# A new order for the attention stage of an attention and expert kernel: loads by turns, experts chosen from tile 0, identity products at the start

## The chip, the cores and the metric

The kernel runs on one core of a Trainium2 chip. The metric is the device time of one execution in microseconds (us); the time shown is the median of three executions.

## What is computed

For each of two batches, x (512 tokens by 1024) passes a cross attention without softmax and then a mixture of experts, each added to x:

```
x = x + matmul(fake_quant(layernorm(x)), fake_quant(ctx))       # ctx: 1024 x 1024 per batch, 8 bit codes
h = layernorm(x)
ratio  = mean|h[tokens 153..511]| / mean|h[tokens 0..152]|        # one number per batch
scores = softmax([h, ratio] @ gate_w + gate_b)                    # 3 experts
top_val, top_idx = top_k(scores, 2), top_val normalised to sum 1
for i in 0, 1:
    j = top_idx[:, 0, i]                                          # the expert that TOKEN 0 of the batch picks
    x = x + top_val[..., i] * (act_j(h @ w1[j] + b1[j]) @ w2[j] + b2[j])
```

Two facts matter for the change. The experts of a batch are those of its token 0, which lies in token tile 0; the other tokens' scores are only used as weights of the outputs. And the ratio needs the absolute values of all tokens of the batch.

## The kernel before, in words

Each batch has four tiles of 128 tokens. All queues are written out by hand, one list of calls for each engine, and semaphores tie them together; an engine takes its list strictly in order.

The **first stage** computes the attention. SyncE loads eight tiles of x (`load_x(i)`, tiles 4 to 7 are batch 1) and sixteen chunks of the context (`load_ctx(c)`, chunks 8 to 15 are batch 1), 512 KB each, through one queue in the order written. A tile of x gets its statistics on VectorE (`x_stats`), its reciprocal deviation on GpSimd (`x_rstd`), its scales on VectorE (`q1_scales`), is turned into codes (`quant_x`), is transposed by TensorE (`transpose_q1`) and is copied out of PSUM (`load_q1T`). A chunk of context is turned into codes by `quant_ctx`. The tables `CTX_ORDER`, `Q1_ORDER`, `Q1T_ORDER` and `H_ORDER` say which engine does which tile. `codes_product(b, t, k)` is two matmuls of 512 columns, for token tile t and context chunk k; `column_sums` and `row_sums` feed `col_term`, `row_term` (ScalarE) and `split_col_term`, `split_row_term` (VectorE), whose result `add_terms(b, t)` adds at the end of a tile. `attn_add(b, t)` (VectorE) then adds the tile to x.

For batch 0 the same stage prepares the experts: `h_stats`, `h_power`, `h_offset`, `h_tile`, `transpose_h`, `split_h` (high part, ScalarE), `h_lo` (low part, VectorE), `sum_h` (absolute values, ScalarE), `sum_abs` and `router_bias` (the ratio), `gate_product(0, t)` (16 small matmuls a tile: the router's logits), `gate_logits`, `gate_turn`, `turned_scores`, `score_steps`, `gate_exp`, `choose_experts`. SyncE waits for the choice, loads `w1` of the chosen expert in quarters of two chunks, and each chunk is split into a rounded part (`w_hi_chunk`, ScalarE) and a rest (`w_lo_chunk`, VectorE) before TensorE may use it.

The **second stage** is a loop over p = 0 to 3 (batch 0 first and second expert, batch 1 first and second expert). Each p has eight blocks f of 24 matmuls (line 1655) and seven products i of 2 x 12 matmuls (line 1623), all of 512 columns. Block f = 0 takes the four chunks of the first two quarters of w1 in turn, six matmuls for each chunk. Beside them VectorE splits weights and activations, adds the second bias (`bias_add`, from `b2row`), adds results (`result`), and for batch 1 computes the router by dot products (`gate_dot(n)`, one for each tile and expert, 12 in all) since batch 1's h is transposed only late: `second_h_tile(t)` (GpSimd) writes h into `b2row`, once both biases of batch 0 have been added, and TensorE transposes it (`transpose_h(1, 0)`) in front of block f = 6 of p = 1. GpSimd also issues the DMAs that add weight regions to each other (`t3_sum`, `t2_sum`, `t4_sum`).

## Time and the profile before

| | before |
|---|---|
| median of 3 runs | 399.26 us (398.29 to 399.35) |
| profiled execution: span, and its own time | 398.3 us, 398.3 us |
| TensorE busy | 384.2 us, 96% |
| VectorE busy | 319.4 us, 80% |
| ScalarE busy | 194.6 us, 49% |
| GpSimd busy | 75.4 us, 19% |
| DMA moved | 66.98 MB, mean 168 GB/s |

The profile is one execution. The span runs from the first to the last instruction. A busy time adds up the time in which an engine works; the records of matmuls overlap, so that the distance from one start to the next says more of TensorE's pace than the length of a record. PE is TensorE, PEld its weight loads, DVE VectorE, ACT ScalarE, POOL GpSimd, SPq the queue of SyncE.

### The profile page before, as it was taken

The numbers are of one execution on the slowest core, as the hardware profiler recorded it, in microseconds if no ns is written. First come the engines' busy times: TensorE is split into PE (matmuls) and PEld (weight loads), VectorE is DVE, ScalarE is ACT, GpSimd is POOL, SyncE is SP. The second block draws the span as 40 slices with busy tenths as digits, with TensorE's granted clock in tenths as the row PEclk, the third lists the DMA queues.
The fourth block names the chain that finished last, engine by engine and source line by source line (L and its number), as shares of the span: only waits on it lengthen the run. The fifth ranks groups of instructions, "written<-read, shape, count | busy, mean of one in ns | idle before, by whom it ended". The sixth has DMA issues, their size and how long they took to land.

```text
span 398.3 us, 5246 instructions
## 1 busy us (share of the span) xinstructions
PE 384.2 (96%) x1860; PEld 302.7 (76%) x1860; DVE 319.4 (80%) x529; ACT 194.6 (49%) x253; POOL 75.4 (19%) x94
## 2 busy tenths in 40 slices
PE   1999999999999999999999999999999999999996
PEld 1345656888888888888888888888888888888885
DVE  8689967999599799898899995654997864639972
ACT  3477745274247635372755833344475244424720
POOL 8647500352110001063103001030000010110000
PEclk9999999999999999999999999999999999999999
DMA  8997019719654676728002898965065884550112
GB/s 300 412 410 305 3 50 375 264 21 282 121 105 137 233 229 226 180 39 158 15 0 90 304 291 281 248 118 96 0 209 172 262 275 88 105 106 2 53 53 107
DMA packets 27437, 66.98 MB, mean 168 GB/s; under 512 B 2160, under 2 KB 2192, under 8 KB 27280
## 3 DMA queue, kind: packets, MB, share of 16 engines
q1 hardware_dynamic: 23888, 54.01, 38.8%
q0 software_dynamic: 3456, 12.58, 16.5%
q8 instruction: 15, 0.25, 0.3%
q14 instruction: 14, 0.11, 0.1%
q10 hardware_dynamic: 64, 0.02, 0.0%
HBM read 49.83 MB, written 4.19 MB: 136 GB/s over the span
## 4 chain that ended last, share of the span: by engine, by line
PE 89%; DVE 6%; POOL 1%; issue 1%; ACT 1%; POOLq 0%; ACTq 0%
PE ps L1655 44%; PE ps L1623 38%; PE ps L1415 4%; DVE bn L840 2%; DVE xres L911 2%; PE ps L1449 1%; POOL ctxq L453 1%; PE ps L1403 1%; DVE hT_lo L920 0%; DVE ctxq L858 0%; POOL ctxq L446 0%; DVE q L874 0%; POOL q_rstd L427 0%; DVE q_bias L1147 0%; PE ps L1484 0%
## 5 line engine op out<-in xcount | busy, mean ns | idle before, releaser
L1037 DVE TENSOR_TENSOR w_lo<-raw,w_hi 128x1024 fp32r<-128x1024 f32 x88 | 103.4, 1218 | 2.6 <-ACT w_hi L688 2.4
L688 ACT ACTIVATE w_hi<-raw 128x1024 fp32r<-128x1024 f32 x88 | 87.8, 1052 | 34.5 <-DVE raw L1050 18.0
L1655 PE MATMUL ps<-hT_hi,w_hi 128*128 128x512 f32 x256 | 100.0, 391 | 0.0
L1655 PE MATMUL ps<-hT_lo,w_hi 128*128 128x512 f32 x256 | 99.6, 389 | 0.0
L1655 PE MATMUL ps<-hT_hi,w_lo 128*128 128x512 f32 x256 | 99.6, 389 | 0.0
L1623 PE MATMUL ps<-w_hi,a_hi 128*128 128x512 f32 x224 | 87.4, 390 | 0.0
L1623 PE MATMUL ps<-w_hi,a_lo 128*128 128x512 f32 x224 | 87.2, 389 | 0.0
L1623 PE MATMUL ps<-w_lo,a_hi 128*128 128x512 f32 x224 | 87.1, 389 | 0.0
L776 ACT ACTIVATE act_f<-ps,b1T 128x512 f32<-128x512 f32 x32 | 22.1, 689 | 112.4 <-PE ps L1655 112.4
L523 POOL DMA_DIRECT2D raw<-raw x24 | 21.3, 1038 | 193.0 <-DMA raw<-in_L_ffn_w_dram 137.9
L1655 PEld LDWEIGHTS ps<-hT_hi,w_hi 128*128 128x128 f32 x256 | 48.1, 188 | 10.6 <-issue 0.4
L1655 PEld LDWEIGHTS ps<-hT_hi,w_lo 128*128 128x128 f32 x256 | 48.1, 188 | 10.1
L1655 PEld LDWEIGHTS ps<-hT_lo,w_hi 128*128 128x128 f32 x256 | 48.1, 188 | 9.7
L1054 DVE TENSOR_TENSOR a_lo<-act_f,a_hi 128x256 fp32r<-128x256 f32 x32 | 15.2, 474 | 47.0 <-ACT a_hi L782 47.0
L1623 PEld LDWEIGHTS ps<-w_hi,a_lo 128*128 128x128 f32 x224 | 42.0, 188 | 8.8
L1623 PEld LDWEIGHTS ps<-w_hi,a_hi 128*128 128x128 f32 x224 | 42.1, 188 | 8.6
L1623 PEld LDWEIGHTS ps<-w_lo,a_hi 128*128 128x128 f32 x224 | 42.1, 188 | 8.6
L1415 PE MATMUL ps<-ctxq,q1T 128*128 128x512 f16 x128 | 32.9, 400 | 1.6 <-DVE xres L911 1.1
L1119 DVE SCALAR_TENSOR_TENSOR xres<-ps,minus_gate,xres 128x512 f32<-128x512 f32 x32 | 23.3, 744 | 8.1 <-PE ps L1623 8.1
L1415 PEld LDWEIGHTS ps<-ctxq,q1T 128*128 128x128 f16 x128 | 11.7, 101 | 18.0 <-issue 5.8
L716 ACT ACTIVATE a_hi<-act_f 128x1024 fp32r<-128x1024 f32 x16 | 16.9, 1058 | 10.8 <-PE ps L1623 10.8
L1103 DVE SCALAR_TENSOR_TENSOR xres<-b2row,gate,xres 128x1024 f32<-128x1024 f32 x16 | 20.5, 1279 | 0.0
(155 smaller groups left out, 367.9 us busy)
## 6 DMA issues: line engine op xcount, KB each, us to landing
raw<-in_L_ffn_w_dram SPq DMA_DIRECT2D x64, 512.0 KB, 5.2
raw<-raw POOLq DMA_DIRECT2D x24, 512.0 KB, 6.6
raw<-in_ctx_dram SPq DMA_DIRECT2D x16, 512.0 KB, 11.8
xres<-in_x_dram SPq DMA_DIRECT2D x8, 512.0 KB, 9.7
out_dram<-xres SPq DMA_DIRECT2D x16, 256.0 KB, 4.1
b2row<-in_L_ffn_b_dram SPq DMA_DIRECT2D x4, 512.0 KB, 6.0
gate_rows<-in_L_ffn_gate_w_dram SPq DMA_DIRECT2D x1, 1536.0 KB, 17.7
small<-in_L_xattn_x_scale_dram ACTq DMA_DIRECT2D x2, 0.0 KB
```

What stands on the lines that cost most here:

```text
L523: G.dma_start(region(into)[:, 2 * c:2 * c + 2, :], region(other)[:, 2 * c:2 * c + 2, :], accum_op=ALU.add).then_inc(done, 16)
L688: nc.scalar.activation(w_hi[n % SLOTS][:, 2 * c:2 * c + 2, :], region(q)[:, 2 * c:2 * c + 2, :], ACT.Copy).then_inc(w_hi_ready, 1)
L716: nc.scalar.activation(dst[:], src, ACT.Copy).then_inc(late_hi_ready, 1)
L776: nc.scalar.activation(act_f[:, f, :], ps[:, G1_BANK + f % 2, :], EXPERT_ACT[ee], bias=bias)
L840: last = V.bn_stats(bn[:, n, c, :], src[:, c * H:(c + 1) * H])
L1037: V.tensor_tensor(w_lo[n % SLOTS][:, 2 * c:2 * c + 2, :], region(n % QUARTERS)[:, 2 * c:2 * c + 2, :], w_hi[n % SLOTS][:, 2 * c:2 * c + 2, ...
L1054: V.tensor_tensor(a_lo[f // TT][:, f % TT, :], act_f[:, f, 0:2 * P], a_hi[f // TT][:, f % TT, :].bitcast(F32), ALU.subtract).then_inc(a_lo ...
L1103: V.scalar_tensor_tensor(out=xt, in0=b2row[:], scalar=gate[:, p * TT + t:p * TT + t + 1], in1=xt, op0=ALU.mult, op1=ALU.add).then_inc(b2_u ...
L1119: V.scalar_tensor_tensor(out=xt, in0=ps[:, bank + j, :], scalar=signed[:, p * TT + t:p * TT + t + 1], in1=xt, op0=ALU.mult, op1=ALU.add).t ...
L1415: T.matmul(ps[:, ATT_BANK[b][t] + c, :], q1T[b][:, k, t * P:(t + 1) * P], ctxq[b][:, k, c * H:(c + 1) * H], start=k == 0, stop=False)
L1623: last = T.matmul(ps[:, bank + j, :], a[slot][:, k, tok], v[w][:, k, :], start=fresh and n == 0, stop=n == 3 * TT - 1, skip_group_check=True)
L1655: last = T.matmul(ps[:, G1_BANK + f % 2, :], w[q % SLOTS][:, k % TT, fs], h[:, k, :], start=n == 0, stop=n == 3 * KT - 1)
```

## The change

- **Loads.** Context chunks and x tiles go by turns: x0 x1 c0 x2 c1 x3 c2 c3 x4 c4 x5 c5 c6 c7 x6 x7 c8 to c15. Before: x0 to x3, c0 to c7, x4 x5, c8 c9, x6 x7, c10 to c15.
- **Experts from tile 0.** For batch 0 only tile 0's logits are computed by `gate_product` and turned (one matmul in `gate_turn` where there were four). The scores of the tiles 1 to 3, and `gate_values`, move into the second stage and use `gate_dot(b, t, e)`: nine dots in p = 0 for batch 0, three in p = 1 (tile 0 of batch 1) and nine in p = 2. Before there were three in p = 0 and nine in p = 1, all for batch 1.
- **Bias.** `bias_add` of the first expert of a batch moves into the blocks f = 0 and 1 of the second expert, whose own bias follows in f = 2 and 3. `b2row` of the second expert is loaded behind all of its weights, and waits for the first bias to be added.
- **Statistics of batch 1's h** (`h_stats(5..7)`) move from p = 0 to p = 1, and GpSimd's `h_power(4..7)` with them, behind the weight sums of p = 0 and ahead of those of p = 1.
- **Identity products.** `keep_busy(n)` issues n matmuls of 128 columns of the identity with ones; their result is not used. They stand ahead of the scales (34), the gate weights (30), and around the first two transposes (8, 10, 24).
- **Order.** The lists of all engines in the first stage, the PSUM banks and the waits that guard them are written anew. The work of the second stage is otherwise the same.

The diff, cut to its core (the banks, their waits and the scores' slices are left out):

```diff
-CTX_ORDER = {"act": [5, 8, 10, 11, 15, 14],
-             "dve": [2, 4],
-             "pool": [0, 1, 3, 6, 7, 9, 12, 13]}
-Q1_ORDER = {"act": [0, 1, 3, 4],
-            "dve": [2, 7],
-            "pool": [5, 6]}
-Q1T_ORDER = {"act": [0, 1, 2, 5, 4, 7],
-             "dve": [3, 6]}
+CTX_ORDER = {"act": [1, 3, 5, 8, 12, 15],
+             "dve": [2, 7],
+             "pool": [0, 4, 6, 10, 11, 9, 14, 13]}
+Q1_ORDER = {"act": [0, 1, 6, 7],
+            "dve": [2],
+            "pool": [3, 4, 5]}
+Q1T_ORDER = {"act": [0, 1, 2, 3, 4, 5, 6, 7],
+             "dve": []}
 H_ORDER = {"act": [],
-           "dve": [],
-           "pool": [0, 1, 2, 3]}
+           "dve": [3],
+           "pool": [0, 1, 2]}
...
-EARLY_DOTS = 3
+DOTS_BEFORE = [NE * (TT - 1), NE * TT, NE * (2 * TT - 1)]
...
+FIRST, OTHERS = slice(0, 1), slice(1, TT)
+WARM_BANK = 5
+WARM_FIRST = 34
+WARM_NEXT = 30
+WARM_GAP = 8
+WARM_WAIT = 10
+WARM_LAST = 24
...
+            def load_b2(p, e):
+
+                if p:
+                    sp.wait_ge(b2_used, TT * p)
+                if p == TOP_K:
+                    sp.wait_ge(hT_ps, B * TT)
+                sp.dma_start(b2row[:], b2[bass.ds(e, 1), :].to_broadcast([P, D])).then_inc(b2_in, 16)
...
             load_x(0)
             load_x(1)
+            load_ctx(0)
             load_x(2)
+            load_ctx(1)
             load_x(3)
-            load_ctx(0)
-            load_ctx(1)
             load_ctx(2)
             load_ctx(3)
+            load_x(4)
             load_ctx(4)
+            load_x(5)
             load_ctx(5)
             load_ctx(6)
             load_ctx(7)
-            load_x(4)
-            load_x(5)
+            load_x(6)
+            load_x(7)
             load_ctx(8)
             load_ctx(9)
-            load_x(6)
-            load_x(7)
             load_ctx(10)
             load_ctx(11)
...
+                if p % TOP_K == 0:
+                    load_b2(p, e)
                 load_w1(p, 2, e)
                 load_w1(p, 3, e)
                 for q in range(4):
                     load_w2(p, q, e)
+                if p % TOP_K:
+                    load_b2(p, e)
                 if p == TOP_K:
                     store_results(sp, 0)
...
+            t3_sum(0)
+            t2_sum(0)
+            t4_sum(0)
             for t in range(TT):
                 h_power(TT + t)
                 h_offset(TT + t)
...
-            t3_sum(0)
-            t2_sum(0)
-            t4_sum(0)
             t3_sum(1)
             second_h_tile(0)
             t2_sum(1)
...
+            load_bias()
+            load_q1T(2)
+            load_q1T(3)
             quant_ctx(5)
-            quant_x(3)
-            load_q1T(2)
+            row_term(0)
             col_term(0)
-            row_term(0)
             quant_ctx(8)
-            quant_x(4)
-            quant_ctx(10)
-            quant_ctx(11)
+            load_q1T(4)
+            load_q1T(5)
+            quant_x(6)
+            quant_x(7)
+            load_q1T(6)
+            quant_ctx(12)
             sum_h(0, 0)
-            load_q1T(5)
+            load_q1T(7)
             split_h(0, 0)
-            load_bias()
             sum_h(0, 1)
-            load_q1T(4)
             split_h(0, 1)
+            gate_logits()
             sum_h(0, 2)
-            quant_ctx(15)
             split_h(0, 2)
-            quant_ctx(14)
             sum_h(0, 3)
             split_h(0, 3)
-            gate_logits(0)
-            load_q1T(7)
-            gate_exp(0)
+            quant_ctx(15)
             row_term(1)
             col_term(1)
+            gate_exp(0, FIRST, 1)
             w_hi_chunk(0, 0)
             w_hi_chunk(0, 1)
             w_hi_chunk(1, 0)
...
                     dve.wait_ge(b2_in, 16 * p + 16)
-                    dve.wait_ge(y2_done, 2 * NP * p)
+                    dve.wait_ge(y2_done, 2 * NP * (p // TOP_K * TOP_K + 1))
...
                     n = 2 * NP * p + 2 * i + j
-                    if i == 0:
+                    if i == 0 and p % TOP_K:
                         dve.wait_ge(b2_used, TT * p + TT)
+                    elif i == 0:
+                        dve.wait_ge(dots_done, NE * (TT * (p // TOP_K + 1) - 1))
                     elif i in (1, 4, 5):
...
-            term_constants()
             x_stats(2)
+            x_stats(3)
             quant_ctx(2)
-            x_stats(3)
-            quant_ctx(4)
             gate_weights()
             q1_scales(2, 2)
             quant_x(2)
-            load_q1T(3)
             x_stats(4)
             x_stats(5)
+            term_constants()
+            q1_scales(4, 2)
+            quant_ctx(7)
+            split_row_term(0)
+            x_stats(6)
             split_col_term(0)
-            split_row_term(0)
-            q1_scales(4, 2)
+            x_stats(7)
             attn_add(0, 0)
+            q1_scales(6, 2)
+            attn_add(0, 1)
             h_stats(0)
-            attn_add(0, 1)
             attn_add(0, 2)
             h_stats(1)
             attn_add(0, 3)
+            h_stats(2)
             h_lo(0, 0)
-            h_stats(2)
             h_stats(3)
             h_lo(0, 1)
-            x_stats(6)
-            x_stats(7)
+            h_tile(3)
             h_lo(0, 2)
-            q1_scales(6, 2)
-            quant_x(7)
             tokens_abs(0)
             h_lo(0, 3)
-            load_q1T(6)
             router_bias(0)
+            split_row_term(1)
             turned_scores()
-            score_steps()
+            score_steps(FIRST)
+            split_col_term(1)
             choose_experts(0)
-            split_row_term(1)
-            split_col_term(1)
             attn_add(1, 0)
             attn_add(1, 1)
+            h_stats(4)
+            attn_add(1, 2)
             w_lo_chunk(0, 0)
             w_lo_chunk(0, 1)
             w_lo_chunk(1, 0)
             w_lo_chunk(1, 1)
-            attn_add(1, 2)
-            gate_values(0)
             attn_add(1, 3)
-            h_stats(4)
             for p in range(PAIRS):
                 q = QUARTERS * p
-                if p == 1:
...
+                        if f < 2:
+                            gate_dot(0, 1, 2 * f)
+                        if f == 0:
+                            gate_dot(0, 1, 1)
+                        elif f == 1:
+                            gate_dot(0, 2, 0)
+                            gate_dot(0, 2, 1)
+                        elif f == 3:
+                            gate_dot(0, 2, 2)
+                        elif f == 4:
+                            gate_dot(0, 3, 0)
+                        elif f == 5:
+                            gate_dot(0, 3, 1)
+                            gate_dot(0, 3, 2)
+                    elif p == TOP_K:
+                        if f == 0:
+                            gate_dot(1, 1, 0)
+                        elif f == 1:
+                            gate_dot(1, 1, 1)
+                            gate_dot(1, 1, 2)
+                        elif f == 2:
+                            gate_dot(1, 2, 0)
+                            gate_dot(1, 2, 1)
+                        elif f == 3:
+                            gate_dot(1, 2, 2)
+                            gate_dot(1, 3, 0)
+                        elif f == 4:
+                            gate_dot(1, 3, 1)
+                        elif f == 5:
+                            gate_dot(1, 3, 2)
+                    elif f < 2:
+                        bias_add(p - 1, 2 * f)
+                        bias_add(p - 1, 2 * f + 1)
+                    elif f < 4:
+                        bias_add(p, 2 * f - 4)
+                        bias_add(p, 2 * f - 3)
+                    if p % TOP_K == 0 and f == 5:
+                        dot_scores(p // TOP_K, OTHERS)
+                        score_steps(OTHERS)
+                    if p == 1:
+                        if f < 3:
+                            h_stats(TT + 1 + f)
+                        elif f == 5:
+                            gate_dot(1, 0, 0)
+                            gate_dot(1, 0, 1)
+                            gate_dot(1, 0, 2)
                     if f == 3:
                         w_lo_quarter(q + 4)
                     elif f == 4:
...
                         router_bias(1)
-                        dot_scores()
-                        score_steps()
...
                                         start=n == 0, stop=n == 2 * KT - 1)
                         n += 1
-                if t == TT - 1:
-                    last.then_inc(logitT_ps, 1)
+                last.then_inc(logitT_ps, 1)
 
             def sum_abs(b):
 
...
+            def keep_busy(n):
+
+                for _ in range(n):
+                    T.matmul(ps[:, WARM_BANK, 0:P], ident_b[:], ones_b[:], start=True, stop=True)
+
             pe.wait_ge(const_ready, 7)
+            keep_busy(WARM_FIRST)
             pe.wait_ge(scales_in, 16 * 4)
             T.matmul(ps[:, CONST_BANK, 0:4], ones[0:1, :], small[0:1, 0:4], start=True, stop=True
                      ).then_inc(scales_ps, 1)
+            keep_busy(WARM_NEXT)
             turn_gate_weights()
+            keep_busy(WARM_GAP)
             transpose_q1(0)
+            keep_busy(WARM_WAIT)
             transpose_q1(1)
+            turn_bias()
+            keep_busy(WARM_LAST)
             codes_product(0, 0, 0)
             codes_product(0, 0, 1)
             codes_product(0, 0, 2)
             codes_product(0, 1, 0)
+            codes_product(0, 1, 2)
             codes_product(0, 1, 1)
             codes_product(0, 0, 3)
-            codes_product(0, 1, 2)
+            transpose_q1(2)
             codes_product(0, 1, 3)
-            codes_product(0, 1, 4)
+            transpose_q1(3)
             column_sums(0, 0)
             column_sums(0, 2)
+            codes_product(0, 2, 0)
+            codes_product(0, 2, 4)
             codes_product(0, 0, 4)
+            row_sums(0)
...
+            transpose_q1(4)
             codes_product(0, 2, 2)
+            add_terms(0, 0)
...
+            codes_product(0, 3, 0)
+            codes_product(0, 3, 7)
             add_terms(0, 2)
+            transpose_q1(6)
...
-            transpose_q1(4)
-            transpose_q1(5)
+            transpose_q1(7)
             transpose_h(0, 0)
-            turn_bias()
+            codes_product(1, 0, 0)
+            codes_product(1, 2, 0)
+            codes_product(1, 2, 4)
+            codes_product(1, 0, 2)
+            transpose_h(0, 1)
+            gate_product(0, 0)
+            codes_product(1, 2, 3)
+            transpose_h(0, 2)
+            codes_product(1, 2, 2)
+            codes_product(1, 0, 3)
+            codes_product(1, 0, 4)
+            transpose_h(0, 3)
+            codes_product(1, 2, 1)
+            codes_product(1, 0, 1)
+            row_sums(1)
+            codes_product(1, 2, 6)
+            column_sums(1, 0)
+            column_sums(1, 2)
+            sum_abs(0)
+            column_sums(1, 4)
+            column_sums(1, 6)
+            codes_product(1, 0, 5)
+            codes_product(1, 0, 6)
+            gate_turn()
             codes_product(1, 1, 0)
-            codes_product(1, 1, 1)
             codes_product(1, 1, 2)
             codes_product(1, 1, 3)
+            codes_product(1, 1, 1)
             codes_product(1, 1, 4)
+            codes_product(1, 0, 7)
+            add_terms(1, 0)
             codes_product(1, 1, 5)
...
+            add_terms(1, 1)
+            codes_product(1, 3, 0)
+            codes_product(1, 2, 7)
             codes_product(1, 2, 5)
-            codes_product(1, 2, 6)
-            add_terms(1, 0)
-            codes_product(1, 2, 7)
-            add_terms(1, 1)
+            codes_product(1, 3, 3)
             add_terms(1, 2)
-            codes_product(1, 3, 0)
+            codes_product(1, 3, 5)
+            codes_product(1, 3, 4)
+            codes_product(1, 3, 6)
+            codes_product(1, 3, 7)
             codes_product(1, 3, 1)
             codes_product(1, 3, 2)
```

## Rows read from the trace of the kernel before

**Rows 1.** The page: the span.
```profile
span 398.3 us, 5246 instructions
```

**Rows 2.** Busy time by stretches: first stage, p = 0, p = 1 (stretch, its length, engines, PEclk, DMA).
```profile
12.07:64.08 52.01, 50.04 (x363) 26.14 (x364) 42.20 (x99) 32.07 (x42) 23.12 (x31) 1.00 0.62 243
64.08:146.14 82.06, 82.06 (x363) 67.54 (x361) 72.52 (x109) 43.17 (x53) 14.47 (x18) 1.00 0.62 181
146.14:231.62 85.48, 85.48 (x395) 71.12 (x394) 80.42 (x131) 46.38 (x65) 17.47 (x10) 1.00 0.50 140
```

**Rows 3.** Timeline of TensorE, 8 to 18 (start, length, instruction, [idle before <-releaser]).
```profile
8.89 0.59 PE L1491 MATMUL ps<-small,ones 1*128 1x6 f32 x2 [2.32 <-DMA b1n<-in_L_ffn_b_dram]
...
16.55 0.15 PEld L1415 LDWEIGHTS ps<-ctxq,q1T 128*128 128x128 f16 x1 [0.28 <-issue]
16.91 1.18 PEld L1415 LDWEIGHTS ps<-ctxq,q1T 128*128 128x128 f16 x6 [0.20 <-issue]
```

**Rows 4.** Timeline of TensorE, 20 to 64: codes, gate products, turn.
```profile
23.84 3.20 PE L1415 MATMUL ps<-ctxq,q1T 128*128 128x512 f16 x14
...
40.85 0.41 PE L1463 MATMUL ps<-hT_hi,gw_parts 128*8 128x128 f32 x1
...
41.94 0.22 PE L1463 MATMUL ps<-hT_lo,gw_parts 128*8 128x128 f32 x1
...
51.73 1.05 PE L1484 MATMUL ps<-pick_logit,b2row 8*128 8x4 f32 x8 [0.21 <-ACT b2row L656]
```

**Rows 5.** Timeline of all engines, 52 to 68: from the scores to the first weights.
```profile
52.90 0.48 DVE L968 TENSOR_SCALAR sc<-ps,gbias 128x4 f32<-128x4 f32 x3 [1.69 <-PE ps L1484]
...
55.32 0.15 DVE L1007 SCALAR_TENSOR_TENSOR expert<-pick 1x1 int32<-1x1 f32 x1
...
56.52 2.19 SPq L329 DMA_DIRECT2D raw<-in_L_ffn_w_dram  x4
...
61.61 1.23 DVE L1037 TENSOR_TENSOR w_lo<-raw,w_hi 128x1024 fp32r<-128x1024 f32 x1 [0.33 <-ACT w_hi L688]
...
64.08 0.50 PE L1655 MATMUL ps<-hT_hi,w_hi 128*128 128x512 f32 x1
...
65.76 2.51 DVE L1037 TENSOR_TENSOR w_lo<-raw,w_hi 128x1024 fp32r<-128x1024 f32 x2 [1.50 <-ACT w_hi L688]
...
67.04 0.19 PEld L1655 LDWEIGHTS ps<-hT_hi,w_hi 128*128 128x128 f32 x1 [0.37 <-DVE w_lo L1037]
```

**Rows 6.** Timeline, 15 to 17: chunks 4 and 5 of the context, quantised as they land.
```profile
15.68 0.82 DVE L865 TENSOR_SCALAR ctxq<-raw,qc,qp 128x1024 uint8<-128x1024 f32 x1 [0.31 <-DMA raw<-in_ctx_dram]
...
16.95 1.24 ACT L566 ACTIVATE ctxq<-raw,qp,qc 128x1024 uint8<-128x1024 f32 x1 [4.02 <-DMA raw<-in_ctx_dram]
```

**Rows 7.** Groups of VectorE, 12 to 64 (busy us, mean ns of one | idle before).
```profile
L840 DVE BATCH_NORM_STATS2 bn<-xres 128x6 f32<-128x512 f32 x18 | 11.4, 676 | 0.0
L911 DVE SCALAR_TENSOR_TENSOR xres<-ps,qc,xres 128x512 f32<-128x512 f32 x12 | 8.2, 734 | 0.7 <-PE ps L1424 0.7
L920 DVE TENSOR_TENSOR hT_lo<-ps,hT_hi 128x512 fp32r<-128x512 f32 x8 | 5.1, 679 | 0.3 <-ACT hT_hi L642 0.2
```

**Rows 8.** Groups of VectorE in the second stage, 64 to 398: bias and dots.
```profile
L1103 DVE SCALAR_TENSOR_TENSOR xres<-b2row,gate,xres 128x1024 f32<-128x1024 f32 x16 | 20.5, 1279 | 0.0
L957 DVE SCALAR_TENSOR_TENSOR ps<-xres,mvh,gate_rows 128x1024 f32<-128x1024 f32 x12 | 19.1, 1593 | 0.4
```

**Rows 9.** Groups of GpSimd, 8 to 64: an h tile of batch 0.
```profile
L481 POOL TENSOR_SCALAR hbuf<-xres,h_rstd,h_shift 128x1024 f32<-128x1024 f32 x4 | 4.8, 1196 | 0.5 <-POOL h_shift L440 0.3
```

**Rows 10.** Timeline of p = 1, 145 to 180: last bias, h tile, its transposes.
```profile
169.99 1.28 DVE L1103 SCALAR_TENSOR_TENSOR xres<-b2row,gate,xres 128x1024 f32<-128x1024 f32 x1
...
171.38 4.59 POOL L473 TENSOR_SCALAR b2row<-xres,h_rstd,h_shift 128x1024 f32<-128x1024 f32 x1 [12.80 <-DVE xres L1103]
...
178.78 1.03 PE L1449 MATMUL ps<-ident,b2row 128*128 128x128 f32 x8
```

**Rows 11.** Tile b2row, its four loads.
```profile
DMA to landing us min/median/max: 4.3/6.0/8.3
```

356 lines of the change are left out of this document (144 added, 212 removed).

## The prediction

> **What bounds the kernel now.** I read the busy time by stretches first. TensorE is busy for the whole of p = 0 and p = 1, and for 50.04 of the 52.01 us of the first stage [rows 2]. The second stage is 60 blocks of 24 matmuls; p = 0 takes 82.06 us for 15 of them, 5.47 us a block, which is the engine's own pace. So whatever the change does before the first expert matmul at 64.08 [rows 5] comes out at the end one for one, unless a wait appears later. The sum is made on the profiled execution, 398.3 us [rows 1]; the median lies 1.0 above it, and I carry the difference over.
>
> Second, the timeline around that start. Three things meet there. TensorE finishes its attention work at 64.08. The first rest chunk of w1 begins at 61.61 and lasts 1.23, so it was ready at 62.84: TensorE was the later one, by 1.2 us. But the third chunk was ready only at 67.0, and TensorE waited 0.37 us for it [rows 5]. So both paths end almost together, and the change must shorten both.
>
> **TensorE's own work in the first stage.** Removed: three of four gate products. One takes from 40.85 to 42.0 [rows 4], 1.15 us; three give 3.4. Of the turn, six of eight instructions, 1.05 us for all [rows 4]: 0.8. Moved to where TensorE had been waiting: the bias turn, 0.2. The clock: the rows print a granted clock of 1.00 for the stretch, the 2.4 GHz level, but the weight loads of 512 column products stand 0.43 us apart until 16.55 and 0.21 apart from 16.91 on [rows 3], with products since 12.07. About ten of these matmuls stood at the slow pace, 2.1 us at 0.21 each. The identity products put work ahead of them, from the moment GpSimd has made its constants.
>
> The fill: 34 + 30 + 8 + 10 + 24 = 106 products of 128 columns. By the 512 column spacing a quarter of 0.43 or 0.21 is 0.11 or 0.055 us each. The first 34 and 30 take at most 6.8 us together, in a time in which TensorE has nothing but the scales to do: it idled 2.32 us until the gate weights landed at 8.89 [rows 3]. Only 8 + 10 + 24 = 42 stand in front of useful work: 2.3 us fast, 4.6 us slow. In the fast case I get the first codes at 13.0 (before: 12.07, and then slow). Chunk 2 lands at 13.1 and the fourth product waits for a copied tile until 14.2, so 0.9 us later costs nothing. In the slow case codes begin near 16.5, 3 us late.
>
> **Loads.** Chunk 4 was read as it landed at 15.68, chunk 5 at 16.95 [rows 6]: 1.27 us a transfer. Chunk 5 was the tenth. In the new order chunk 0 is third (8.0, before 10.5), x3 sixth (11.8, before 9.3), chunk 7 fourteenth (22.05, before 19.5), x7 sixteenth (24.6, before 27.2). Batch 0 is complete 2.5 us later, batch 1's x earlier.
>
> **VectorE from chunk 7 on.** Its list from 22.05 to the end of `h_lo(0,3)` is: one chunk (0.82, [rows 6]), two term splits, six statistics, four `attn_add`, four `h_lo`, `h_tile(3)` and scales. By the means of [rows 7]: six statistics at 2 x 0.68 + 0.1 are 8.7, four adds at 2 x 0.73 are 5.9, four `h_lo` at 2 x 0.68 are 5.4; the rest with the chunk is about 3.9. Sum 23.9, so 45.95 with no wait. Walking the three lists side by side I find 0.7 us of waits (column term, the halves of `h_lo`): 46.7. Before, the ratio's matmul waited for the same `h_lo(0,3)` until 49.7. The order puts row sums and two column sums ahead of that matmul, 47.4; router bias 48 to 49; the turned matmul waits for the products ahead of it on TensorE, done at 50.0. Before, scores began at 52.90, and the expert was known at 55.47 [rows 5]. That span, 2.57, stays; `split_col_term(1)` now sits in it and costs 0.45 beyond the wait it fills. Expert at 53.1, 2.4 us earlier. From there to the weights nothing changes: 1.05 to the issue at 56.52, and 6.32 to the first rest chunk at 62.84 [rows 5]. New: 60.5, and the third chunk, which had been ready at 67.0, at 64.6.
>
> **TensorE to the start.** After the turn at 50.0 there are 19 code products of 2 matmuls (14 matmuls in 3.20 us [rows 4], less the overlap of the last, 0.217 each: 8.25 us) and four term additions (about 0.53 each, 2.1): start at 60.6. Weights at 60.5. Block f = 0 then meets the third chunk at 64.6 (it needs it at 63.3) and has 12 matmuls left at 5.44 / 24: end 67.35. Before: 67.04 + 2.8 = 69.85. **Gain at the end of f = 0: 2.5 us**, not the 3.5 of the start, since the weights still arrive at their own pace.
>
> **The second stage.** p = 0: a dot costs 1.59 + 0.14 and its gap, 1.77 us; a bias 1.28 [rows 8]. Nine dots (15.9) and the scores (3.5) replace three dots, three statistics and four biases (14.8) and the gate values (1.9). VectorE was busy 72.5 of 82.1 us there [rows 2], so 2.7 more fits. Its tightest place: after block f = 1's three dots the chunks for f = 4 are ready from 82.2; f = 4 starts at 83.7. Cost 0, margin 1.5. p = 2 takes nine dots in place of four biases, in a stretch with over 20 us of VectorE slack; p = 3 the same with biases. Cost 0. The tail is unchanged.
>
> p = 1 is different. VectorE was busy 80.4 of 85.5 us [rows 2]. What matters is the last of eight biases there, since `second_h_tile(0)` may write `b2row` only behind it. Before: last bias 169.99, ended 171.2; h tile 171.38 to 175.97; TensorE wants it at 178.78 [rows 10], a margin of 2.8 us. After, in the same times: the first expert's biases end at 163.3, only then is the second `b2row` requested. Its load takes 4.3 to 8.3 us [rows 11]; nothing else is in flight, so I take 4.3: 167.7. Statistics and biases follow, last bias 174.8, 3.6 later. GpSimd meanwhile has `h_power(7)` (behind the statistics at 171.5) and `t3_sum(1)` ahead of the tile, which free it at about 175 to 178. The tile itself took 1.20 us in the first stage [rows 9] and 4.59 here [rows 10]. I take 3 us from 176: ready 179 to 180, **a stall of 0.9 us** before the transposes of f = 6, between 0 (a tile of 1.2) and 5.3 (4.59 after late work, and a load of 6.0).
>
> Why the same tile takes 1.20 or 4.59 the rows do not say; VectorE was working beside it throughout. The Trainium skill, "SBUF — State Buffer", the section on its two physically separate sides, states that a VectorE instruction with two SBUF inputs and a GpSimd instruction that reads SBUF exclude each other by a lock held for the whole instruction. By that rule the tile, which would now start beside the splits of f = 3 and 4, waits as it did before, 4.6 us, and the stall would be 2 us and more.
>
> **Sum.** -2.5 + 0.9 = -1.6 us: 396.7 for the profiled execution, 397.7 for the median.
>
> **The rivals.**
> - **R1, forecast:** start near 60.6, f = 0 fed by the weights, a stall under 1.8 us in p = 1. 396.8 to 398.6. Chance 0.40.
> - **R2, more gained:** the p = 1 stall is absent, and the expert comes another 1 us earlier, because my walk gave VectorE's waits too much. 399.3 - 3.5 = 395.8. For it: the three lists have no other break that I see, and TensorE's bound alone (52.0 us less 3.4, 0.8, 0.2, 2.1, and 1 to 2 of waits) would let it start at 57 to 58. Against: then the weights are the limit. Chance 0.20.
> - **R3, the fill hurts:** the pace stays slow until the first codes, the 42 products cost 4.6 us, codes begin 3 us late, and since column sums and VectorE meet at 25 with no slack, most of it reaches the expert. Gain at f = 0 about 0, with the stall 399.3 to 400. Against: the slow pace ended 4.8 us after 12.07 [rows 3], and the fill is at work far more than that before 13. Chance 0.12. The Trainium skill, "TensorE: Matmul & The Clock Gate", part 1, has the clock rise once TensorE has been kept at work. The last parts of the fill would then be fast, and the sum stays as above; by its other half, that idle time lets the clock fall, the waits between them would speak for R3.
> - **R4, slower:** the h tile of p = 1. The point is a stall of 2.5 us: `b2row` later than 4.3 and the tile at 4.59. At 6.0 and 4.59 the stall is 5.3: 399.3 - 2.5 + 5.3 = 402. For it: the load's median is 6.0 and the same tile did take 4.59 in this place. Against: those 6.0 us had weight loads ahead of them in the queue. Chance 0.18; the lock of the page named above works towards this one, and the two rows of the tile bear it out only in part.
> - **R5, no gain:** the chain to the expert is late on ScalarE (its list from 25.9 to the row term has 23 us of work for 23 us of time), so the expert comes at 55 as before. 399 to 399.8. Chance 0.10.
>
> **Chances.** 0.3% is 1.2 us, about what a measurement of this kernel can tell from no change. Faster by more: R2 and four fifths of R1, 0.53. Within: the rest of R1, R5, half of R3 and a little of R4, 0.25. Slower: 0.22. The likeliest case has 396.8 to 398.6; with R2 below and the milder half of R4 above the range is 395.3 to 401.
>
> **What would show it.** The first 512 column products 0.21 apart from the start (R3: 0.43). First expert matmul at 60 to 61, `expert` written near 53, an idle of about 1.3 us inside f = 0 put down to `w_lo`. In p = 1 an idle before the transposes of `b2row` put down to GpSimd; its size decides between R1, R2 and R4. Wrong would be: an idle elsewhere in the second stage, above all before f = 4 of p = 0 or product i = 3 of p = 1 (VectorE late); or an expert later than 54.

## The result and the profile after

The changed kernel takes **397.28 us** (median of 5 runs, 396.88 to 397.70) against 399.26 us (398.29 to 399.44) for the kernel before on the same chip: ratio 0.9954, 95% interval 0.9942 to 0.9967. In a later session it took 397.65 us (9 runs, 397.01 to 398.68) against 399.22: 0.9966 (0.9954 to 0.9978). So it is 0.4% faster, 1.6 to 2.0 us; the forecast was 397.7.

In every run with both numbers the time is 1.7 to 1.8 us above the span. The table ahead gives 398.3 as span and as own time of the profiled execution of before; by this offset that execution took about 400.0, more than any of the five times of its session. So the spans [rows 1] and below differ by 3.1 us, the medians by 2.0. I therefore profiled the kernel before a second time (span 397.2) and the changed kernel a second time (span 395.9).

The page of the changed kernel, and its busy time in the three stretches of [rows 2] (stretch, its length, then busy time and instructions of PE, PEld, DVE, ACT, POOL, the granted clock, DMA share, GB/s):

```profile
span 395.2 us, 5413 instructions
...
PE 388.2 (98%) x1912; PEld 305.7 (77%) x1912; DVE 337.1 (85%) x575; ACT 201.9 (51%) x261; POOL 75.8 (19%) x94
```

```profile
13.20:60.27 47.07, 45.86 (x311) 21.70 (x309) 43.05 (x111) 32.50 (x43) 25.21 (x31) 1.00 0.62 246
60.27:142.20 81.93, 81.93 (x360) 67.48 (x361) 73.50 (x118) 45.95 (x57) 7.19 (x9) 1.00 0.61 180
142.20:228.50 86.30, 86.00 (x395) 71.07 (x394) 80.22 (x131) 45.99 (x65) 23.23 (x19) 1.00 0.51 143
```

Read against [rows 2]: the first stage is 4.94 us shorter though it begins 1.13 later, p = 0 is 0.13 shorter, and p = 1 is **0.82 us longer**. The kernel before has 81.78 and 85.49 for p = 0 and p = 1 in its second profile. What was won at the start is not kept whole.

The start, on the timeline of TensorE, 2 to 16:

```profile
2.20 3.81 PE L1549 MATMUL ps<-ones_b,ident_b 128*128 128x128 f16 x34 [2.20 <-POOL vis_text L431]
...
11.85 1.51 PE L1549 MATMUL ps<-ones_b,ident_b 128*128 128x128 f16 x24
13.20 3.26 PE L1458 MATMUL ps<-ctxq,q1T 128*128 128x512 f16 x14
```

Fourteen products of 512 columns in 3.26 us, 0.22 apart from the first one on; before, they stood 0.43 apart at first [rows 3].

From the scores to the first weights, timeline of all engines, answering to [rows 5]:

```profile
49.92 0.47 DVE L984 TENSOR_SCALAR sc<-ps,gbias 128x1 f32<-128x1 f32 x3
...
52.60 0.15 DVE L1029 SCALAR_TENSOR_TENSOR expert<-pick 1x1 int32<-1x1 f32 x1
...
53.80 2.19 SPq L336 DMA_DIRECT2D raw<-in_L_ffn_w_dram  x4
...
58.91 1.21 DVE L1062 TENSOR_TENSOR w_lo<-raw,w_hi 128x1024 fp32r<-128x1024 f32 x1
...
61.91 2.57 DVE L1062 TENSOR_TENSOR w_lo<-raw,w_hi 128x1024 fp32r<-128x1024 f32 x2 [0.31 <-ACT w_hi L700]
```

```profile
59.73 0.50 PE L1467 MATMUL ps<-term_cols,term_rows 64*128 64x512 f32 x2
60.27 0.47 PE L1700 MATMUL ps<-hT_hi,w_hi 128*128 128x512 f32 x1
```

The expert is written at 52.60 (before at 55.32), the first rest chunk is ready at 60.12, and the first expert matmul starts at 60.27. The third chunk is ready at 63.1. In the second profile of the changed kernel TensorE is the one that waits here:

```profile
61.17 0.47 PE L1700 MATMUL ps<-hT_hi,w_hi 128*128 128x512 f32 x1 [0.22 <-DVE w_lo L1062]
```

Then p = 1, VectorE and GpSimd, and TensorE's weight loads:

```profile
163.12 2.48 DVE L1129 SCALAR_TENSOR_TENSOR xres<-b2row,gate,xres 128x1024 f32<-128x1024 f32 x2 [1.71 <-DMA b2row<-in_L_ffn_b_dram]
...
170.30 3.41 POOL L487 TENSOR_SCALAR b2row<-xres,h_rstd,h_shift 128x1024 f32<-128x1024 f32 x1
...
172.71 1.26 DVE L1091 TENSOR_TENSOR act_f<-act_f 128x256 f32<-128x256 f32 x1
...
176.54 1.77 POOL L534 DMA_DIRECT2D raw<-raw  x2 [2.83 <-DVE w_lo L1062]
...
177.43 2.40 DVE L1103 SCALAR_TENSOR_TENSOR act_f<-act_f 128x256 f32<-128x256 f32 x1
177.71 1.84 POOL L487 TENSOR_SCALAR b2row<-xres,h_rstd,h_shift 128x1024 f32<-128x1024 f32 x1
...
221.59 2.34 DVE L1062 TENSOR_TENSOR w_lo<-raw,w_hi 128x1024 fp32r<-128x1024 f32 x2
```

```profile
216.99 0.19 PEld L1673 LDWEIGHTS ps<-w_hi,a_hi 128*128 128x128 f32 x1 [0.27 <-issue]
222.91 0.19 PEld L1673 LDWEIGHTS ps<-w_hi,a_hi 128*128 128x128 f32 x1 [0.63 <-issue]
```

```profile
222.94 0.47 PE L1673 MATMUL ps<-w_hi,a_hi 128*128 128x512 f32 x1 [0.23 <-DVE w_lo L1062]
```

The transposes of f = 6 start on time, 32.64 us after the start of p = 1 (before 32.65). The loss is at the start of the products i = 5 (0.30 us) and i = 6 (0.35): the matmul at 222.94 is put down to `w_lo`, whose chunk for i = 6 VectorE began at 221.59. VectorE, which waited 1.71 us for `b2row` and spent 2.40 on an instruction that takes 0.42, shows no rest from 163 to 229.

**A ledger of the first stage.** I add up the distances from each matmul's start to the next, by kind, from the first codes to the first expert matmul (us):

| | before | before, second | after | after, second |
|---|---|---|---|---|
| first codes at | 12.07 | 11.68 | 13.20 | 12.72 |
| products of codes (128) | 31.12 | 30.69 | 30.58 | 30.52 |
| gate products | 4.41 | 4.41 | 0.97 | 0.97 |
| turn of the scores | 1.20 | 1.20 | 0.31 | 0.31 |
| bias turn | 0.94 | 0.94 | 0 | 0 |
| all the rest | 14.34 | 14.33 | 15.21 | 16.65 |
| first expert matmul at | 64.08 | 63.25 | 60.27 | 61.17 |
| second block at | 69.92 | 68.87 | 66.04 | 66.74 |

A distance holds whatever comes before the next start, so a wait of the next instruction is booked on the kind ahead of it. The row of the code products must be read with that. The first 18 matmuls of codes of the kernel before took 6.13 and 5.71 us from the first start to the last, where the fast pace of 0.217 would give 3.7. The first 14 of the changed kernel took 2.87 and 2.81, which is that pace. So the slow start is gone in full, 2.4 and 2.0 us. The other 1.9 us went to waits that follow later code products, above all this one, in every profile of the changed lists, for the h tile that the change gave to VectorE (`h_tile(3)`):

```profile
43.72 1.09 PE L1497 MATMUL ps<-ident,hbuf 128*128 128x128 f32 x8 [0.56 <-DVE hbuf L898]
```

### The profile page after: what moved, and what is told of

Same layout as the page of the kernel before. It is cut to its first block, busy times and chain, and to the rows that moved or that the text cites. A ratio compares the mean times of both kernels' runs of the same rounds, so it can differ in the third digit from the quotient of the medians.

```text
span 395.2 us, 5413 instructions
## 1 busy us (share of the span) xinstructions
PE 388.2 (98%) x1912; PEld 305.7 (77%) x1912; DVE 337.1 (85%) x575; ACT 201.9 (51%) x261; POOL 75.8 (19%) x94
## 4 chain that ended last, share of the span: by engine, by line
PE 82%; DVE 11%; DMA 3%; issue 2%; SPq 1%; POOL 1%; DVEq 0%; POOLq 0%
PE ps L1700 44%; PE ps L1673 32%; PE ps L1458 3%; DMA xres<-in_x_dram 3%; DVE xres L1147 2%; DVE w_lo L1062 2%; DVE bn L856 2%; DVE xres L927 1%; DVE hT_lo L936 1%; PE ps L1497 1%; SPq L325 1%; SPq L330 1%; DVE a_lo L1119 1%; PE ps L1467 0%; DVE hbuf L898 0%
## 5 line engine op out<-in xcount | busy, mean ns | idle before, releaser
L1700 PEld LDWEIGHTS ps<-hT_hi,w_hi 128*128 128x128 f32 x256 | 48.1, 188 | 10.7 <-DVE w_lo L1062 0.5
L1079 DVE TENSOR_TENSOR a_lo<-act_f,a_hi 128x256 fp32r<-128x256 f32 x32 | 13.3, 417 | 26.1 <-ACT a_hi L796 26.1
L973 DVE SCALAR_TENSOR_TENSOR ps<-xres,mvh,gate_rows 128x1024 f32<-128x1024 f32 x21 | 33.5, 1594 | 1.3
L1458 PE MATMUL ps<-ctxq,q1T 128*128 128x512 f16 x128 | 31.1, 380 | 0.3 <-DVE xres L927 0.3
L728 ACT ACTIVATE a_hi<-act_f 128x1024 fp32r<-128x1024 f32 x16 | 16.9, 1056 | 10.3 <-PE ps L1673 10.3
```

Of the source, the lines that this page charges most:

```text
L728: nc.scalar.activation(dst[:], src, ACT.Copy).then_inc(late_hi_ready, 1)
L973: V.scalar_tensor_tensor(out=ps[:, X_BANK:X_BANK + 2, :].rearrange("p a n -> p (a n)"), in0=xres[:, i, :], scalar=mvh[:, i, 0:1], in1=gate ...
L1079: V.tensor_tensor(a_lo[f // TT][:, f % TT, :], act_f[:, f, 0:2 * P], a_hi[f // TT][:, f % TT, :].bitcast(F32), ALU.subtract).then_inc(a_lo ...
L1458: T.matmul(ps[:, ATT_BANK[b][t] + c, :], q1T[b][:, k, t * P:(t + 1) * P], ctxq[b][:, k, c * H:(c + 1) * H], start=k == 0, stop=False)
L1700: last = T.matmul(ps[:, G1_BANK + f % 2, :], w[q % SLOTS][:, k % TT, fs], h[:, k, :], start=n == 0, stop=n == 3 * KT - 1)
```

## The experiments

Ratios are to the kernel before in the same session. I give three places of each profile: the first expert matmul, the length of p = 0 from its second block on, and that of p = 1. The second is 76.16 to 76.23 in all fourteen profiles, so a difference comes from the first stage (with f = 0) or from p = 1.

| run | time, runs | ratio (95%) | start | p = 1 |
|---|---|---|---|---|
| before, second profile | 398.91, 1 | | 63.25 | 85.49 |
| changed, again | 397.65, 9 | 0.9966 (0.9954 to 0.9978) | 61.17 | 86.33 |
| e1 no identity products | 396.99, 12 | 0.9938 (0.9920 to 0.9956) | 62.79 | 85.48 |
| e2 old order of loads | 402.39, 4 | 1.0070 (1.0044 to 1.0097) | 66.52 | 85.95 |
| e3 statistics early | 398.05, 9 | 0.9981 (0.9951 to 1.0012) | 61.55 | 86.32 |
| e4 biases early | 397.48, 6 | 0.9957 (0.9943 to 0.9971) | 61.57 | 85.77 |
| e5 last group left out | 398.01, 6 | 0.9972 (0.9959 to 0.9985) | 61.24 | 86.10 |
| e6 twelve more matmuls | 400.23, 6 | 1.0031 (1.0016 to 1.0046) | 63.60 | 86.42 |
| e7 before, new loads | 401.02, 10 | 1.0042 (1.0026 to 1.0057) | 65.44 | 85.49 |
| e8 before, identity products | 399.68, 10 | 1.0011 (0.9992 to 1.0030) | 64.86 | 85.48 |
| e9 e4 and dots early | 397.04, 6 | 0.9939 (0.9916 to 0.9962) | 61.03 | 85.48 |
| e10 e9 without identity products | 396.65, 6 | 0.9931 (0.9908 to 0.9954) | 60.91 | 85.49 |

**The first session: two references and three edits.**

> The kernel before once more, for a second profile. Between the profiles the spans differ by 3.1 us, between the medians the times by 2.0. Theory A (the first profile of before was a slow execution: its third chunk of w1 landed 2.8 us after the second, and 1.4 us would be the pace of the others): here that gap is near 1.4, the wait at 67.0 is gone, and the span is 397.2 to 397.7. Rival B (the gap belongs to the kernel, the bias row load stands between the chunks): the gap is 2.8 again, and the span near 398.3.

Its first 18 matmuls of codes took 6.09 us (6.50 in the other profile). What differed beside that is when the chunks of w1 land. ScalarE's timeline in it:

```profile
59.72 1.06 ACT L688 ACTIVATE w_hi<-raw 128x1024 fp32r<-128x1024 f32 x1 [3.45 <-DMA raw<-in_L_ffn_w_dram]
61.06 1.06 ACT L688 ACTIVATE w_hi<-raw 128x1024 fp32r<-128x1024 f32 x1 [0.28 <-DMA raw<-in_L_ffn_w_dram]
62.69 1.06 ACT L688 ACTIVATE w_hi<-raw 128x1024 fp32r<-128x1024 f32 x1 [0.57 <-DMA raw<-in_L_ffn_w_dram]
```

From the second chunk to the third it is 1.63 us. In the profile that I predicted from the gap was so long that VectorE waited 1.50 us before the third (the last but one row of [rows 5]). The gap is not in every execution, but it is not a single case either: the third chunk landed 2.78, 1.69, 1.34 (e7) and 2.32 (e8) us behind the second in the four profiles with the lists of before, and 1.34 to 1.61 in the ten with the new lists. Whether the new lists shorten it or chance does is open.

**e1, no identity products.**

```diff
-WARM_FIRST = 34
-WARM_NEXT = 30
-WARM_GAP = 8
-WARM_WAIT = 10
-WARM_LAST = 24
+WARM_FIRST = WARM_NEXT = WARM_GAP = WARM_WAIT = WARM_LAST = 0
```

> The changed kernel with no identity products at all; the rest is as it is. Theory A (the fill buys the fast pace for the first codes, and TensorE's path is tight): the 512 column products stand 0.43 us apart until near 16.8, some five to eight of them now lie in that time with work waiting, so the start of the expert matmuls moves from 60.3 to about 61.4 and the kernel takes 1.0 us more than the changed one (near 398.3). Rival B (the first codes are paced by the chunks and copied tiles, so the slow pace is hidden): the same time within 0.3 us. Rival C (the fill costs, the first codes began at 13.2 because of it): 0.5 us less.

```profile
12.01 2.08 PE L1458 MATMUL ps<-ctxq,q1T 128*128 128x512 f16 x4 [0.21 <-ACT q1T L632]
14.60 4.45 PE L1458 MATMUL ps<-ctxq,q1T 128*128 128x512 f16 x10 [0.51 <-DVE ctxq L881]
```

The codes were slow past 18.4 in this profile (10 in 4.45 us), and the start came 1.6 to 2.5 us later than with the products. The expert, too, was known later, at 55.15 (52.75 and 53.48), and TensorE waited for the first rest chunk. Its time was 398.43, the second slowest of twelve (395.82 to 399.32); the median was no worse than the changed kernel's, so this profile is not the usual case. p = 1 lost nothing.

**e2, the changed kernel with the order of loads of before** (x0 to x3, c0 to c7, x4 x5, c8 c9, x6 x7, the rest).

> The changed kernel with the load order of before (x0 to x3, c0 to c7, x4 x5, c8 c9, x6 x7), all lists of the engines left. Theory A (loads by turns is what lets VectorE do the statistics of x4 and x5 while it waits for chunks): x4 arrives 5 us later, VectorE stands in front of it, and everything behind, the expert too, comes 3 to 4 us later: 3 us more than the changed kernel, slower than before. Rival B (the order of loads matters little, the queues catch up by 40 us): within 0.5 us of the changed kernel.

```profile
26.49 0.61 PE L1446 MATMUL ps<-ctxq,ones_b 128*32 128x512 f16 x2 [3.57 <-POOL ctxq L467]
```

```profile
22.00:30.00 8.00, 4.18 (x15) 1.23 (x13) 7.66 (x26) 3.44 (x5) 5.61 (x5) 0.79 1.02 408
```

The first is TensorE's timeline, the second the windows of 22 to 30. GpSimd's list asks for x tiles 4 and 5 before chunk 6 and sat idle for 6.05 us, since they were loaded late; TensorE waited 3.6 us for that chunk. The granted clock is 0.79 on the mean of this stretch: behind the wait TensorE ran at the 1.2 GHz level until 29.7, with its 512 column products 0.43 us apart. The new lists with the old loads are slower than before: the order of loads is worth 4.7 to 5.1 us beside them.

**e3, three statistics earlier.** `h_stats(5)` and `(6)` go ahead of results 4 and 5 of p = 0, `(7)` to f = 0 of p = 1.

```diff
-                        if f < 3:
-                            h_stats(TT + 1 + f)
+                        if f == 0:
+                            h_stats(TT + 3)
```

> The changed kernel with two of the three statistics of batch 1's h taken out of p = 1 and put where VectorE idled at the end of p = 0 (ahead of results 4 and 5). Theory A (VectorE's surplus in p = 1 is what makes TensorE wait 0.3 us at product 5 and 0.35 at product 6 of p = 1): with 2.9 us less work there those waits vanish, p = 2 starts 0.7 to 0.8 us earlier against the start of p = 1, and the kernel takes 0.7 us less (near 396.6). Rival B (the waits come from ScalarE or the h tile of GpSimd, not from VectorE's amount of work): no change within 0.3 us.

```profile
166.73 2.48 DVE L1129 SCALAR_TENSOR_TENSOR xres<-b2row,gate,xres 128x1024 f32<-128x1024 f32 x2 [4.91 <-DMA b2row<-in_L_ffn_b_dram]
```

A miss: p = 1 stayed at 86.32. What VectorE no longer did before the second bias it spent waiting for `b2row`, 4.91 us instead of 1.71. The load of that row may start only when the first expert's fourth bias has read it. That gave the next theory.

But most of that wait is not this dependence. The row took 6.21 us from issue to landing, against 3.72 in the changed kernel. With the statistics gone from p = 1 GpSimd's list moved up as well, and its first weight sum of p = 1 was issued beside the row's load (at 160.50) instead of 6 us behind its landing:

```profile
159.22 1.83 POOL L534 DMA_DIRECT2D raw<-raw  x2
```

So e3 is no test of the amount of VectorE's work by itself; that the two transfers slowed each other is likely and not shown.

**The second session: the changed kernel, and three edits of it.**

> The changed kernel again, as the reference for the three others of this call. Expected 397.3 us, as in its first measurement (396.9 to 397.7). The start of the expert matmuls is expected within 0.5 us of 60.3, since its first products of codes ran at the full clock from the start; the kernel before varied by 0.8 us there between two profiles (64.08 and 63.25).

It started 0.9 later than in its first profile: 0.70 and 0.88 between two matmuls at 20.4 and 30.8, where it waited for a chunk and for an x tile's codes, are in this profile and not in the other.

**e4, all four biases of the first expert ahead of p = 1's first activation** (and likewise in p = 3).

```diff
                     k = f - TT
+                    if p % TOP_K and f == 0:
+                        for t in range(TT):
+                            bias_add(p - 1, t)
                     dve.wait_ge(act_ready, p * KT + f + 1)
...
-                    elif f < 2:
-                        bias_add(p - 1, 2 * f)
-                        bias_add(p - 1, 2 * f + 1)
-                    elif f < 4:
+                    elif 2 <= f < 4:
```

> The four bias additions of the first expert are put at the head of the second expert's pass, before the wait for its first activation (the last two stood behind the second activation). Theory C: in the second expert's pass VectorE is the engine that is short of time; it lost 1.71 us waiting for the row b2row of the second expert, whose load may start only when the fourth of those additions has read the row. With the additions 9 us earlier that wait is gone, VectorE has a rest before the last products, and the 0.8 us that TensorE lost at products 5 and 6 come back: first matmul of the third pass 85.5 us after the first of the second (86.3 now), time 396.5 us, 0.8 below the changed kernel. Rival D: not VectorE's amount of work but the order of the last products' weights (ScalarE's high halves, the slots' release by TensorE) sets those waits; then the pass stays at 86.3 and the time at 397.3.

VectorE's timeline, its rests in p = 1:

```profile
161.03 0.43 DVE L1079 TENSOR_TENSOR a_lo<-act_f,a_hi 128x256 fp32r<-128x256 f32 x1 [2.43 <-ACT a_hi L796]
...
162.52 2.48 DVE L1129 SCALAR_TENSOR_TENSOR xres<-b2row,gate,xres 128x1024 f32<-128x1024 f32 x2 [0.60 <-DMA b2row<-in_L_ffn_b_dram]
...
177.36 0.42 DVE L1079 TENSOR_TENSOR a_lo<-act_f,a_hi 128x256 fp32r<-128x256 f32 x1 [1.32 <-ACT a_hi L796]
```

In the trace 0.56 of the 0.84 came back (86.33 to 85.77, where the kernel before has 85.49). The medians (397.48 against 397.65) don't resolve it.

**e5, the last 24 identity products left out.**

```diff
-WARM_LAST = 24
+WARM_LAST = 0
```

> The last group of identity products, 24 before the first product of codes, is left out; the other 82 stay. In the changed kernel the first codes start at 13.20, in the one without any filling at 12.01 but at half the clock until 19. Theory E: TensorE keeps its clock over the short gap, the codes start at 12.0 and run at full speed, and as TensorE then waits for context chunks some of the 1.2 us is lost again: start of the expert matmuls 0.3 to 1.2 earlier, time 396.3 to 397.0. Rival F: the first codes wait for their chunks anyway, so that the start does not move and the time is 397.3. Rival G: the clock falls in the gap and the start is later by 2, time 399.

```profile
13.58 0.59 PE L1458 MATMUL ps<-ctxq,q1T 128*128 128x512 f16 x2
14.62 2.90 PE L1458 MATMUL ps<-ctxq,q1T 128*128 128x512 f16 x12 [0.45 <-ACT ctxq L580]
```

The pace held (2.90 us for 12, 0.23 apart, behind a wait), so G falls. But the gate weights landed late in this execution (their turn at 10.8, not 9.3), so that the codes did not start earlier and the start is no test of E's 12.0; the codes then waited for a chunk as F has it. The ratio and that of the changed kernel lie in each other's intervals.

**e6, twelve more matmuls in TensorE's list, behind the turn of the scores** (the attention of batch 1 is changed by them).

```diff
             gate_turn()
+            for _ in range(6):
+                codes_product(1, 0, 6)
```

> Six more calls of one product of codes (12 matmuls of 0.227 us, 2.7 us) stand in TensorE's order right behind the turn of the scores; the second batch's attention result is changed by them. Neither the choice of the experts nor the load of their weights is behind them, TensorE is. Theory A: after the change TensorE's own order sets the start of the expert matmuls: they start 2.7 later less the 0.25 that it waited for the third chunk, and 0.8 us of it come back in the second expert's pass, where VectorE is then less far behind: time +1.7, 399.0 us. Rival B: the weights set the start and TensorE had time to spare: the start moves by under 1 us and the time is within 0.5 of 397.3.

+2.6 us in time, +2.4 at the start, and nothing given back in p = 1 (86.42). Theory A is right about the start and wrong about the 0.8. But the matmuls did not lie on TensorE's path alone. VectorE's list has `attn_add(1, 2)` ahead of the first rest chunk, and that waits for TensorE's products:

```profile
62.24 4.62 DVE L1062 TENSOR_TENSOR w_lo<-raw,w_hi 128x1024 fp32r<-128x1024 f32 x4
```

ScalarE had that chunk's rounded part done at 59.5; in the second profile of the changed kernel the rest chunk began at 59.80. So e6 delays both paths, and shows that TensorE has almost nothing to spare, not that it is the one that ends last.

**The third session.**

**e7, the kernel before with the new order of loads.**

> The kernel before with the changed kernel's order of loads alone. The changed kernel with the old order of loads was 5.1 us slower than the changed one: x tiles 6 and 7 and chunks 8 and 9 came too late for its TensorE order, which waited 3.95 us at 22.54 and lost clock. Theory A: an order of loads is worth something only beside the order of the work; the engines' lists of before ask for x tiles 2 and 3 first and then the chunks, so the new order brings nothing: time 399.2 (398.5 to 400.5). Rival B: the load order is itself the gain: 397.5. Rival C: the two have to fit as closely here as in the changed kernel and the mismatch costs 3 to 5 us: 402 to 404.

2.0 us slower than before, more than theory A says and less than rival C: in its timeline TensorE waits 0.98 us up to 20.96 for a chunk that ScalarE quantised, and the start is 1.4 to 2.2 later.

**e8, the kernel before with the 106 identity products.**

> The kernel before with the changed kernel's 106 identity products ahead of its first codes (in a free bank), nothing else. Its first 18 codes took 6.50 us in one profile and 6.09 in another, against 4.1 at the full pace of 0.227. Theory A: the filling pays for itself and no more: the codes start 1.2 later and run 2.0 to 2.4 faster, so the start of the expert matmuls is 0.8 to 1.2 earlier and the time 398.2 to 398.4. Rival B: it is worth nothing, since later waits for chunks take up what the faster codes gain, or since the codes in unprofiled runs are not as slow: 399.2. Rival C: it delays, by up to 1.2: 400.4.

```profile
14.21 1.47 PE L1415 MATMUL ps<-ctxq,q1T 128*128 128x512 f16 x6 [0.22 <-DVE ctxq L865]
17.46 1.90 PE L1415 MATMUL ps<-ctxq,q1T 128*128 128x512 f16 x8 [1.78 <-POOL ctxq L453]
```

```profile
16.20 1.20 POOL L453 TENSOR_SCALAR ctxq<-raw,qc,qp 128x1024 uint8<-128x1024 f32 x1 [2.87 <-DMA raw<-in_ctx_dram]
```

Rival B holds in the time: 399.68, nothing gained. The products run at full pace, and the first 18 end no sooner, 19.29 against 18.51 and 17.69. The reason is not settled by this profile. The 1.78 us before 17.46 are a wait for a chunk that landed late in this execution: chunk 3 came at 16.11, 2.79 us behind chunk 2, where it came at 14.37 and 14.00 in the two profiles of before, 1.28 behind it. What the products meet when it lands in time no profile shows.

**e9, e4 with the three gate dots at f = 1, 2 and 4 instead of f = 5; e10, the same without identity products.**

```diff
                         if f < 3:
                             h_stats(TT + 1 + f)
+                            if f:
+                                gate_dot(1, 0, f - 1)
-                        elif f == 5:
-                            gate_dot(1, 0, 0)
-                            gate_dot(1, 0, 1)
+                        elif f == 4:
                             gate_dot(1, 0, 2)
```

> The changed kernel with the early bias additions (the run before: second expert's pass 85.77 us instead of 86.33, with VectorE resting 2.43, 0.60 and 1.32 us before 177.4 and never between 177.4 and 229), and the three gate dots of the second batch's first tile, 4.8 us that stood behind f=5, at f=1, 2 and 4, where those rests are. Theory C: VectorE's amount of work behind f=5 is what is left of the loss: the pass takes 85.5, the time is 0.8 below the changed kernel's 397.3 to 397.65, so 396.5 to 396.9. Rival D: the rest of the loss is not VectorE's; the pass stays at 85.8 and the time at 397.0 to 397.5.

> The same without the 106 identity products. The changed kernel without them measured 396.99, with a spread of 395.8 to 399.3, against 397.28 and 397.65 with them, though its profile started the expert matmuls 1.6 to 2.5 later and gave back nothing in the second pass. Theory A: the filling is worth 1.0 to 1.5 us once the second pass no longer hides it: time 397.5 to 398.0, above the kernel of the run before. Rival B: the filling brings nothing on the mean, and only narrows the spread: 396.5 to 396.9, as the run before, with a wider spread.

p = 1 is back at 85.48 and 85.49, as before the change. e9 took 397.04 and e10 396.65 us. Both medians are below the changed kernel's two, e10's ratio of 0.9931 against 0.9954 and 0.9966, but the intervals overlap, and the kernel before was 0.2 to 0.3 us faster beside these two runs too (398.99); a gain of some 0.5 us over the changed kernel is likely and not shown.

## Why the prediction was right, point by point

**TensorE's own work: right in sum, by errors that cancel.** The ledger gives 3.44 for the gate products (forecast 3.4) and 0.89 for the turn (0.8). The first codes gained 2.4 and 2.0 us of pace in the two pairs of profiles (2.1). The bias turn was 0.94 with what it waited, not 0.2. So the forecast took off 6.5 us, and its start of 60.6 leaves 2.1 for waits; the two pairs have 7.7 and 7.3 off, 2.7 and 4.2 of waits on, and codes that begin 1.1 and 1.0 later (forecast 0.9). First codes 13.0 (13.20 and 12.72), start 60.6 (60.27 and 61.17): right. The [rows 2] clock of 1.00 was no evidence against the slow pace; the last section says why.

**The identity products brought no time in the end, where the forecast counts 2.1 for them.** They put the codes on the full pace, but start them later: at 12.72 to 13.48 in the seven profiles of the new lists that have all of them, at 12.01 and 12.40 in e1 and e10. Behind the first 16 stand the transposes of x tile 3, which wait for GpSimd's codes of that tile until 17.46 in the changed kernel and until 17.57 in e10: there the slow pace was all but hidden. In e1 it lasted to 18.8 and was not. The medians are no worse without the products (e1, and e10 against e9) and no better with them (e8). That they are worth nothing within these intervals is shown; the share of each reason is not.

**The expert: right.** Forecast 53.1, measured 52.75 and 53.48 at the end of its write; scores begin at 49.92 and 50.65 (turned matmul forecast done at 50.0). The gain against before is 2.7 and 1.2 us in the two pairs, forecast 2.4.

**The third chunk: mis-sized, and this is the size that the sum missed at the start.** I let the weights "still arrive at their own pace" with the gap of one execution and forecast f = 0 to end at 67.35. It came at 66.04 and 66.74. The gain there is 3.9 between the two first profiles, 2.1 between the two second ones, 3.0 on the mean, against 2.5. The idle of 1.3 us inside f = 0 that the prediction named as a sign was not there: the block took 5.77 and 5.57 us where 5.44 is the full pace. The sum was made on an execution with the long gap and of about 400.0 us, and its difference was then taken off the median; that the result fits to 0.4 us is in part luck.

**What bounds the start.** "Both paths end almost together": in the kernel before the first expert matmul started 1.2 to 1.3 us behind the end of the first rest chunk (four profiles), and TensorE was the later one. In all ten profiles of the new lists it started 0.14 to 0.15 behind it, with up to 0.35 us of idle time on TensorE. So the rest chunk on VectorE now ends last, and TensorE has at most some 0.3 us to spare. That the change must shorten both is not shown apart: e6 moved both. Nor was the removal of the gate products run alone; their 3.4 us are read from the traces.

**The loads** were worked through in the prediction and given no price. Beside the new lists they are worth about 5 us, and in the lists of before they cost 2 (e2, e7): neither the new order of loads nor the new lists gain anything by themselves.

**p = 0, p = 2, p = 3 at no cost: right**, 76.16 from the second block on, and 81.60 for p = 2 as before.

**p = 1: the right amount by the wrong step.** Forecast a stall of 0.9 before f = 6's transposes, because GpSimd would have the h tile ready at 179 to 180. Measured 0.82, elsewhere; that the two numbers agree is luck. `b2row` landed as forecast (3.7 us; 4.3 taken). GpSimd was free 1.8 us earlier than I took it, 28.1 us into p = 1 and not 29.9: the tile started at 170.30, took 3.41 and was ready at 173.7, 1.1 before TensorE took it. The step that failed is that "VectorE was busy 80.4 of 85.5 us", read and then used only for the order of the biases. With 1.71 lost to `b2row`, 1.98 inside one instruction beside GpSimd's second tile and 0.85 in another beside the first, VectorE finished the low halves for products 5 and 6 too late. The kernel before lost 0.86 beside each of the two tiles, so the tiles cost 1.1 more than they did. And its last rest in p = 1, 1.10 us up to 192.08, lay behind such losses, where the changed kernel's last rest ended at 163.12. Where the split of product 6's chunk begins, in us after the start of p = 1, decides the length of p = 1:

| | split for product 6 begins | p = 1 |
|---|---|---|
| before (both profiles), e9, e10 | 77.92 to 77.96 | 85.48, 85.49 |
| e1 | 78.46 | 85.48 |
| e4 | 78.86 | 85.77 |
| e2 | 79.08 | 85.95 |
| e5 | 79.20 | 86.10 |
| changed (both), e3 | 79.39 to 79.42 | 86.30 to 86.33 |
| e6 | 79.51 | 86.42 |

The profiles of e7 and e8 have 77.93 and 77.94, and 85.49. Up to 78.46 it is free, and from about 78.5 on each us costs about one. This is shown: three edits of VectorE's list (e3, e4, e9) move the one number or leave it, and the other follows. e9 also shows what was needed beside the earlier biases: the dots ahead of the last rest. It also settles two things that I expected wrongly: a later TensorE does not bring the 0.8 back (e6), since VectorE's list starts from TensorE's results; and e1 lost nothing because the long instruction fell otherwise there, not because it was late.

**The lock that I quoted.** What the trace shows is in the rows of VectorE and GpSimd above: the VectorE instruction recorded from 177.43 ends at 179.83, 0.28 us behind GpSimd's tile (177.71 to 179.55), and the one from 172.71 ends at 173.97, 0.27 behind the tile before it (170.30 to 173.71). In all fourteen profiles a VectorE instruction of 1.26 to 1.35 us, usually 0.42, ends 0.27 behind the first tile. In e1 the second tile fell beside a gate dot, which took 2.43 instead of 1.58, and the pair's loss was 0.85 in place of 1.98. The Trainium skill, "SBUF — State Buffer", the section on its two physically separate sides, says that such a pair excludes each other for a whole instruction; the trace agrees. I had applied it to GpSimd alone, whose four tiles take 3.41, 1.84, 3.84 and 5.14 us. It stops VectorE as well, and VectorE was the engine that had no time to give.

**The rivals.** R1 held in number (396.8 to 398.6), with its start and without its stall. R2 had half: no stall at f = 6, but the expert was 0.35 earlier than forecast in one profile and 0.4 later in the other, not 1 earlier. R3 did not happen; R4's point, the late tile, did not come about; R5 neither.
